# Attention probabilities divided and transposed, values as weights, in three of five attentions; one product per bank for a low-rank term

## The reference

```python
x = x + L0_attn(ln(x))           # 16 heads of 16, RoPE, tanh cap at 50, causal
x = x + L0_xattn(ln(x), ctx)     # 16 heads of 64, keys ctx[0:112] through a causal mask
x = x + L0_ffn(ln(x))            # 256-1024-256, gelu, plus low-rank terms
x = x + L1_attn(ln(x))           # 8 query heads, 2 latent key/value heads of 32, causal
x = x + L1_xattn(ln(x), ctx)     # 16 heads of 16, all 375 keys, padding mask
x = x + L1_ffn(ln(x))            # top 2 of 4 experts, each a whole encoder layer
...
m1 = (even[:, :4, :, None] * odd[:, :4, None, :]).reshape(Bx, Hx, Dx)   # from tokens 1..16
h = x @ W1.T + scale * einsum('bsd,bhd->bsh', x, m1) + b1
```

## Time and profile before

| | us |
|---|---|
| median of three runs (lowest, highest) | 3894.98 (3891.59, 3895.25) |
| the profiled execution | 3896.07 |
| its span in the trace | 3894.4 |

### The profile page before, as it was taken

The page is one execution under the profiler, slowest core; times in us unless marked ns, Lnnn a source line. Parts: engine busy times, 40 slices in busy tenths (PEclk is TensorE's granted clock), DMA queues, the critical chain, the costliest instruction groups (busy, mean ns, idle before and its releaser), DMA issues. The chain is left out here.

```text
span 3894.4 us, 81102 instructions
## 1 busy us (share of the span) xinstructions
PE 3612.2 (93%) x32871; PEld 2736.2 (70%) x32871; DVE 1980.3 (51%) x5378; ACT 1434.1 (37%) x3167; POOL 371.6 (10%) x455
## 2 busy tenths in 40 slices
PE   6999999999699898989898989994899999999997
PEld 4777777777576666666666666662788887878886
DVE  3665656566235353535353534452455555556554
ACT  2343344334134233333333343432344443444443
POOL 1111111111000000000000000000011111111111
PEclk9999999999699999999999999997899999999999
DMA  2000000000200001010101010001300001110000
GB/s 76 12 12 13 14 12 12 14 14 8 88 11 13 24 11 25 9 27 9 28 5 31 1 35 1 25 1 54 129 16 12 11 17 50 54 52 12 15 12 8
DMA packets 63555, 94.55 MB, mean 24 GB/s; under 512 B 7762, under 2 KB 59602, under 8 KB 62146
## 3 DMA queue, kind: packets, MB, share of 16 engines
q1 hardware_dynamic: 55074, 83.41, 6.9%
q0 software_dynamic: 8224, 7.36, 1.7%
HBM read 72.07 MB, written 18.37 MB: 23 GB/s over the span
## 5 line engine op out<-in xcount | busy, mean ns | idle before, releaser
L1478 PE MATMUL bps<-BXT,Bwexp 128*128 128x112 f32 x3072 | 379.7, 282 | 6.2 <-DMA Bwexp<-in_we 3.6
L1478 PEld LDWEIGHTS bps<-BXT,Bwexp 128*128 128x128 f32 x3072 | 361.7, 195 | 22.1 <-issue 9.3
L1243 DVE CUSTOM_DVE_ANT_0 PON<-pps,PMR 112x375 f32<-112x375 f32 x512 | 259.7, 544 | 194.3 <-PE pps L967 192.9
L1096 ACT ACTIVATE PPT<-pps,mcol 125x896 f32<-125x896 f32 x192 | 192.4, 1007 | 204.6 <-PE pps L986 204.4
L1564 PE MATMUL bps<-Bwexp,BPT 128*112 128x256 f32 x1024 | 235.9, 380 | 0.0
L657 POOL TENSOR_TENSOR rstd<-var,nhalf 112x1 f32<-112x1 f32 (+1 forms) x96 | 148.3, 1545 | 838.6 <-DVE var L575 459.1
L967 PE MATMUL pps<-PKT,PQM 64*112 64x375 f32 x1024 | 211.1, 501 | 6.0 <-DVE Pmx L1243 4.0
L1276 POOL TENSOR_TENSOR Prstd<-Pvar,nhalf 112x1 f32<-112x1 f32 x128 | 70.1, 548 | 1517.9 <-DVE Pvar L1164 1517.9
L1618 ACT ACTIVATE BPT<-bps,Bwexp 128x112 f32<-128x112 f32 x512 | 139.1, 354 | 170.9 <-PE bps L1478 170.9
L1564 PEld LDWEIGHTS bps<-Bwexp,BPT 128*112 128x112 f32 x1024 | 174.5, 177 | 35.3
L986 PE MATMUL pps<-PQM,PKT 64*125 64x448 f32 x768 | 187.5, 567 | 0.0
(11 more groups left out here) (302 smaller groups left out, 7280.8 us busy)
## 6 DMA issues: line engine op xcount, KB each, us to landing
Bwexp<-in_we SPq DMA_DIRECT2D x7, 2304.0 KB, 17.0
PCX<-in_ctx SPq DMA_DIRECT2D x32, 375.0 KB
BXIN<-xmid SPq DMA_DIRECT2D x64, 112.0 KB
out<-BY POOLq DMA_DIRECT2D x64, 112.0 KB, 2.9
Bwexp<-in_we SPq DMA_DIRECT2D x7, 777.0 KB, 4.6
wa_sb<-in_wa SPq DMA_DIRECT2D x1, 4736.0 KB, 14.8
Brexp<-in_re SPq DMA_DIRECT2D x7, 672.0 KB
XIN<-in_x SPq DMA_DIRECT2D x32, 112.0 KB
```

Of the source, the lines that this page charges most:

```text
L1096: A(PT[s][0:KP, k, :, :].rearrange("p (i v) q -> p i (v q)", i=2), PS[s][0:KP, :, 0:QW], ACT.Exp, bias=mcol[:, k, bass.ds(at.n[s] + s * qu ...
L1243: m = v.tensor_tensor_reduce(out=ON[s][0:T, i * LC:(i + 1) * LC], in0=bank[s][i][0:T, 0:LC], in1=MR[s][:, :], scale=1.0, scalar=-3.0e38, o ...
L1478: m = mm(o[:, j * T:(j + 1) * T], wt[:, c, n0 + j * 128:n0 + (j + 1) * 128], rhs[:, c, :], start=(c == 0), stop=(c == 1))
```

## The change

All three attentions now go the same way, eight heads at a time: scores with queries on the partitions; row maxima on DVE; one exponential for each head on ACT, with the negated maximum as bias and the row's sum as second output (`accum_out`); DVE divides the 112 x 896 probabilities; PE transposes them, ACT copies them; PE multiplies with V as weights and the probabilities moving, which gives the output with features on the partitions. In L0_xattn and L1_attn DVE adds the mask and takes the maximum in one instruction for each head (`tensor_tensor_reduce`), and PE's mask product goes. The transposes of the output go, and in L1_attn and the experts the selecting products and the second scores too. `V48` holds V of two heads with 16 columns of zeros between, so that two products of 32 output rows fill one group of rows. In L0_ffn the tiles of f1 are taken in another order, so that bank g needs one and the same 96-row operand, and the four products become one of 448 columns.

```diff
-    "lead2": (0, 66, 241, 415),
+    "lead2": (0, 341, 505, 677),
...
             t.wait(xf_read[s], 2)
         else:
             t.wait(tp_ready[s])
-        for i in range(2):
-            mm(bank[s][i][0:T, 0:QW], identb, causalb, start=True, stop=True)
         for n in range(4):
             for i in range(2):
                 m = mm(bank[s][i][0:T, n * T:(n + 1) * T], QT[s][side[i], 4 * g + n, :], KX[s][side[i], 4 * g + n, :],
-                       start=False, stop=True, skip_group_check=True)
+                       start=True, stop=True)
         m.then_inc(s_psum[s], 1)
         yield
         t.wait(soft_ready[s])
...
         m.then_inc(pt_psum[s], 1)
         yield
         t.wait(pt_ready[s])
-        for i in range(2):
-            for n in range(4):
-                m = mm(bank[s][i][0:T, 65 * n:65 * n + 65], PT[s][:, 8 + 4 * i + n, :],
-                       V64[s][:, 8 * g + 2 * n + i, :], start=True, stop=True)
+        for n in range(4):
+            for i in range(2):
+                m = mm(b0[side[i], n * T:(n + 1) * T], V64[s][:, 8 * g + 2 * n + i, :], PT[s][:, 8 + 4 * i + n, :],
+                       start=(n == 0), stop=True, skip_group_check=True)
         m.then_inc(o_psum[s], 1)
-        yield
-        t.wait(on_ready[s])
-        transposes(b0, ON[s][:, 512 * g:512 * g + 512], 4).then_inc(tp_psum[s], 1)
...
-        t.wait(sub_ready[s])
-        A(PT[s][:, 0:8, :], PT[s][:, 0:8, :], ACT.Exp).then_inc(soft_ready[s], 1)
+        t.wait(top_ready[s])
+        for h in range(8):
+            m = A(PT[s][:, h, :], PT[s][:, h, :], ACT.Exp, bias=low[s][:, h:h + 1], accum_out=sums[s][:, h:h + 1])
+        m.then_inc(sum_ready[s], 1)
         yield
         t.wait(pt_psum[s])
         A(PT[s][:, 8:16, :].rearrange("p (i n) q -> p i (n q)", i=2), PS[s][0:T, :, 0:QW],
           ACT.Copy).then_inc(pt_ready[s], 1)
         yield
-        copy_transposed(OT[s][:, 4 * g:4 * g + 4, :], b0)
+        t.wait(o_psum[s])
+        A(OT[s][:, 4 * g:4 * g + 4, :], b0[:, 0:QW].rearrange("p (n q) -> p n q", n=4), ACT.Copy).then_inc(tp_ready[s], 1)
...
-        top = mx[s][:, 8 * g:8 * g + 8]
-        scores = PS[s][0:T, :, 0:QW].rearrange("p i (n k) -> p i n k", n=4)
...
+        for i in range(2):
+            for n in range(4):
+                h = 4 * i + n
+                m = v.tensor_tensor_reduce(out=PT[s][:, h, :], in0=bank[s][i][0:T, n * T:(n + 1) * T], in1=causalb[:, 0:T],
+                                           scale=1.0, scalar=-3.0e38, op0=ALU.add, op1=ALU.max, accum_out=mx[s][:, h:h + 1])
+        chained(m)
+        v.tensor_scalar(low[s][:, :], mx[s][:, 0:8], -1.0, None, ALU.mult).then_inc(top_ready[s], 1)
+        yield
+        t.wait(sum_ready[s])
+        chained(v.reciprocal(rec[s][:, 0:8], sums[s][:, :]))
+        v.tensor_tensor(PT[s][:, 0:8, :], PT[s][:, 0:8, :], rec[s][:, 0:8].unsqueeze(2).to_broadcast((T, 8, T)),
+                        ALU.mult).then_inc(soft_ready[s], 1)
...
     def hidden(g):
         for j in range(4):
             for c in range(C2):
-                mm(bank[s][g][:, j * T:(j + 1) * T], f1[:, c, (4 * g + j) * 128:(4 * g + j + 1) * 128], XT[s][:, c, :],
+                mm(bank[s][g][:, j * T:(j + 1) * T], f1[:, c, (2 * j + g) * 128:(2 * j + g + 1) * 128], XT[s][:, c, :],
                    start=(j == 0 and c == 0), stop=False, skip_group_check=True)
         if g == 0:
             t.wait(g_ready[s])
-        for j in range(4):
-            mt = 4 * g + j
-            m = mm(bank[s][g][:, j * T:(j + 1) * T], XN[s][0:32, (mt % 2) * 128:(mt % 2) * 128 + 128], GS[s][:, mt // 2, :],
-                   start=False, stop=True, skip_group_check=True)
+        m = mm(bank[s][g][:, 0:QW], XN[s][0:96, g * 128:(g + 1) * 128], GS[s][:, :, :], start=False, stop=True, skip_group_check=True)
...
-        mm(b1[0:32, 64:64 + T], XT[s][:, c, 1:33], XT[s][:, c, :], start=(c == 0), stop=(c == 1), skip_group_check=True)
+        mm(b1[0:96, 64:64 + T], XT[s][:, c, 1:97], XT[s][:, c, :], start=(c == 0), stop=(c == 1), skip_group_check=True)
...
-    second(range(0, 4))
+    second(range(0, FT, 2))
...
-    second(range(4, 8))
+    second(range(1, FT, 2))
...
     t.wait(la_ready[s], 2)
-    for i in range(2):
-        mm(bank[s][i][0:T, 0:QW], identb, causalb, start=True, stop=True)
     for n in range(4):
         for i in range(2):
             m = mm(bank[s][i][0:T, n * T:(n + 1) * T], QM[s][side[i], n // 2, n % 2, :], KL[s][side[i], n // 2, :],
-                   start=False, stop=True, skip_group_check=True)
+                   start=True, stop=True)
     m.then_inc(s_psum[s], 1)
     yield
-    t.wait(mx_ready[s])
-    mm(b0[0:16, 0:T], MXP[s][:, :], identb, start=True, stop=True).then_inc(mt_psum[s], 1)
-    yield
-    t.wait(mt_ready[s])
+    t.wait(on_ready[s])
     for n in range(4):
         for i in range(2):
-            mm(bank[s][i][0:T, n * T:(n + 1) * T], csel[:, 4 * i + n, :], MV[s][:, :],
-               start=(n == 0), stop=False, skip_group_check=True)
...
+            m = transpose(bank[s][i][0:T, n * T:(n + 1) * T], PF[s][:, 4 * i + n, :], ident[0:T, 0:T])
     m.then_inc(st_psum[s], 1)
+    t.skip(mx_ready[s], 1)
+    t.skip(small_ready[s], 1)
     yield
     t.wait(p_ready[s])
-    for h in range(8):
-        c, j = h // 4, h % 4
-        m = mm(b0[0:T, 33 * h:33 * h + 33], PF[s][:, 4 * (j // 2) + 2 * c + j % 2, :], V32[s][:, c, :], start=True, stop=True)
-    m.then_inc(o_psum[s], 1)
+    for c in range(C2):
+        for j in range(4):
+            m = mm(b0[rows[j], c * T:(c + 1) * T], V32[s][:, c, :], PF[s][:, 4 * (j // 2) + 2 * c + j % 2, :],
+                   start=(c == 0), stop=True, skip_group_check=True)
+    m.then_inc(sp_psum[s], 1)
     token_major(b1[0:KP, 0:D], CT[s][:, :, 2 * KP:3 * KP], yv, 0, D).then_inc(kv_psum[s], 1)
-    yield
-    t.wait(on_ready[s])
-    transposes(ON)
...
-    copy_max(MV[s][0:16, :], b0[0:16, 0:T])
+    t.wait(mx_ready[s])
+    for h in range(8):
+        m = A(PF[s][:, h, :], PF[s][:, h, :], ACT.Exp, bias=neg[s][:, h:h + 1], accum_out=sums[s][:, h:h + 1])
+    m.then_inc(small_ready[s], 1)
     yield
     t.wait(st_psum[s])
-    A(PF[s].rearrange("p (i n) q -> p i (n q)", i=2), PS[s][0:T, :, 0:QW], ACT.Exp).then_inc(p_ready[s], 1)
+    A(PF[s].rearrange("p (i n) q -> p i (n q)", i=2), PS[s][0:T, :, 0:QW], ACT.Copy).then_inc(p_ready[s], 1)
     yield
     t.wait(kv_psum[s])
     A(V16[s][:, 2, :, 0:16], b1[0:KP, 0:D].rearrange("p (h d) -> p h d", h=H), ACT.Copy).then_inc(kv_read[s], 1)
-    copy_transposed(OT)
+    t.wait(sp_psum[s])
+    A(OT[s][:, :, :], b0[:, 0:C2 * T].rearrange("p (c q) -> p c q", c=C2), ACT.Copy).then_inc(tp_ready[s], 1)
...
-            t.wait(mx_ready[s])
+            t.wait(exp_ready[s])
         for v in range(4):
             for i in range(2):
                 m = mm(bank[s][i][0:T, v * T:(v + 1) * T], QM[s][side[i], c, v, :], KT[s][side[i], c, :], start=True, stop=True)
         m.then_inc(s_psum[s], 1)
-    yield
-    t.wait(mx_ready[s])
...
+    for c in range(C2):
+        yield
+        t.wait(soft_ready[s])
         if c == 0:
-            t.wait(mt_ready[s])
+            t.wait(exp_ready[s])
         else:
-            t.wait(p_ready[s])
+            t.wait(pt_ready[s])
         for v in range(4):
             for i in range(2):
-                mm(bank[s][i][0:T, v * T:(v + 1) * T], msel[side[i], 4 * c + v, 0:T], MXT[s][side[i], :],
-                   start=(v == 0), stop=False, skip_group_check=True)
...
+                m = transpose(bank[s][i][0:T, v * T:(v + 1) * T], PT[s][0:T, 8 * c + 4 * i + v, :], ident[0:T, 0:T])
+        m.then_inc(pt_psum[s], 1)
+    yield
+    t.wait(pt_ready[s])
+    for c in range(C2):
+        for n in range(2):
+            for k in range(4):
+                m = mm(b0[32 * k:32 * k + 32, c * T:(c + 1) * T], V48[s][:, 4 * c + k, 16 * n:16 * n + 32],
+                       PT[s][0:T, 8 * c + 2 * k + n, :], start=(c == 0 and n == 0), stop=(n == 1), skip_group_check=True)
+    m.then_inc(o_psum[s], 1)
...
-    t.wait(mt_psum[s])
-    A(MXT[s][:, :], b0[:, 0:T], ACT.Copy).then_inc(mt_ready[s], 1)
...
+    A(V48[s][:, :, :].rearrange("p k (n d) -> p k n d", n=3)[:, :, 0:3:2, :], b0[0:T, 0:D].rearrange("p (k n d) -> p k n d", k=8, n=2),
+      ACT.Copy).then_inc(vx_read[s], 1)
+    for c in range(C2):
+        yield
+        t.wait(top_ready[s])
+        for i in range(2):
+            for v in range(4):
+                h = 8 * c + 4 * i + v
+                m = A(PT[s][0:T, h, :], bank[s][i][0:T, v * T:(v + 1) * T], ACT.Exp, scale=0.25, bias=low[s][:, h:h + 1],
+                      accum_out=sums[s][:, h:h + 1])
+        m.then_inc(exp_ready[s], 1)
+    for c in range(C2):
+        yield
+        t.wait(pt_psum[s])
         A(PT[s][0:T, 8 * c:8 * c + 8, :].rearrange("p (i v) q -> p i (v q)", i=2), PS[s][0:T, :, 0:QW],
-          ACT.Exp, scale=0.25).then_inc(p_ready[s], 1)
-    yield
...
+          ACT.Copy).then_inc(pt_ready[s], 1)
+    yield
```

(3 more changed lines are left out.)

144 lines of the change are left out of this document (48 added, 96 removed), and 82 rows, old and new, of the table TURNS.

## The result

| | before | after |
|---|---|---|
| median of 4 runs, same chip | 3894.14 us (3891.59 to 3895.25) | 3747.80 us (3743.57 to 3758.23) |
| profiled execution, span | 3896.07, 3894.4 | 3746.19, 3744.5 |
| after / before | | 0.9632, interval 0.9619 to 0.9645 |

It is faster, by 146 us where 284 were forecast, and 18 us above the end of the range. The missing half is best looked at by phase. A phase begins with the first PE group of its own: L797 at 1040.76 and L1472 at 2734.74 before, L795 at 978.58 and L1459 at 2577.87 after.

The account below looks back on a forecast made before the run. PE was taken to bound all three phases, the other engines' work lying beside it. From 3896 us came off 284 of PE's work and 1 net for waits, turns and ends: 3611 profiled, 3610 median; 8-in-10 range 3545 to 3730.

Parts of the forecast that it names:

- PE's sum, 284 us: All phases: PE work saved, 95 us in phase 1, 98 in phase 2, 91 in phase 3.
- So small waits remain: 0.2 per item, 13 us: Phase 3: PE's waits in the new order cost 0.2 us per item, 13 us in all.
- The one wait that I had reckoned: Phase 3: an item's second scores wait 4.1 us for the first's exponentials; lane 0 has 4.7 us between its scores.
- Rival B: Phase 3, some in phase 1: exponentials serial on ACT, 0.51 us a head, so PE waits; 3700 us; chance 0.20.
- Filling and draining get longer: 10 us: Phase 2: lanes' leads spread to 0.677 of a round, so filling and draining take 10 us more.
- The turn of phase 1, +5: Phase 1: DVE's loop grows from 168 to 289 instructions; its turn adds 5 us.
- Rival E: Phase 1: DVE's 289-instruction loop stops at each turn as in phase 2; 37 us, 3642 us; chance 0.08.
- The turn of phase 2, -35: Phase 2: work queued ahead takes back a third of each loop turn's cost, 5 us per turn, seven turns, 35 us.
- C: Phase 2: the loop's turn costs nothing any more; 77 us on top, 3533 us; chance 0.07.
- D: PE's new products no cheaper: dear ends in phases 1 and 2, 3701 us; or dear transposes, 3727; chance 0.10 for both.
- the 1.10 in the prediction: Phase 3: selecting products and second scores taken out, 1.10 us, twice per item; set against eight transposes at 0.81.
- F: Phase 3: slower, ACT's chain of maximum, exponentials, division, transposes sets the pace; 3968 us at 0.9 a head; chance 0.03.

Follow-up runs that it names:

- new tables: Changed kernel, same code, with other tables of turns for all five engines in phase 3 alone: 3639.51 us, 0.9342.
- both new orders: Changed kernel with other tables of turns in phase 3 and phase 1's leads all shifted by 195 turns: 3613.01 us, 0.9277.
- the shifted one: Changed kernel with phase 1's leads all 195 turns further, so only the place of the loop's branch moves: 3717.57 us, 0.9557.

## Why the prediction was wrong, point by point

**PE's sum, 284 us: right in its prices, and close by phase.** L430, L424, L837 and L1505 have the places forecast. With new tables an item of phase 3 has (69.59 - 63.29)/4 = 1.58 us less work where 1.42 stood; in phase 2 a round written out has 11.4 less where 12.2 stood. The low-rank groups gave 13 us where 15 stood. PE's busy time as a whole fell by 219 us in the changed kernel and by 267 with both new orders. That the kernel with both orders takes 3613 us, where 3611 was the sum, is partly luck, as shown above.

**"So small waits remain: 0.2 per item, 13 us": the step that failed.** Measured are 4.3 us of idle PE a round, 1.1 an item, 69 in 64 items; the new tables won 105 in phase 3, the starts and ends of the lanes and PE's shorter groups with them. The one wait that I had reckoned, of the second scores for the first group's exponentials, is there and has its size: 0.9 us a round, where 0.8 stood. I took it for the only one. Left out were four others: the first transposes wait for the second group's exponentials (0.8), since these read the bank that the transposes overwrite; the product with V and the product for V wait for copies that stand behind eight heads in ACT's queue (0.7 and 1.0); and PE waits for SP's release of the weights (0.9). A step of ACT that had been one exponential of 0.91 us had become 2.63, and the order left no room for the 1.72 more. So I had asked for one consumer of the heads, and neither for the other nor for those of the steps queued behind them. Rival B had the symptom and nearly the time (3700) but by another cause, a head of 0.51, and that was not so: luck. That ACT's work, at most 12.4 us an item, lies under PE's 15.9 was true (11.7 measured) and proved nothing here. What is shown is that the order makes the waits, since other tables take them away. What share ACT's own queue has in them is argued from the timeline and not shown by a run.

**"Filling and draining get longer: 10 us": mis-sized.** A round of phase 2 is 18.1 us shorter with its turn and 14.8 without, eight rounds 145 or 118; yet the phase won 95, and 79 written out. So what lies outside the rounds grew by 40 to 50 us. The leads leave one lane alone at the end, PE idle a third of the time and then slow for it. Closing the gap won 54, of which the ends themselves are 21 to 24.

**The turn of phase 1, +5: mis-sized.** The step said that it costs PE "at most the 1.54 us in rows 3", plus 5 in all. The six turns cost 25.5 us, 12.4 before, so 13 more. With the branch at another place 24.5 us of phase 1 went. Rival E had 37 more, by a stop of DVE at its 289 instructions: too much, and DVE didn't stop. Another 14 us of phase 1 are missing. PE's waits for the new chain (its transposes for DVE's division L634 11.5 us, its product with V for ACT's copy 4.0, its scores for DVE 3.6) are 19 us, where those of the old transposes and product were 7. Most of the 11.5 lie outside 100 to 950, at the ends of the phase, where one lane is alone with its chain. This was not tried by itself.

**The turn of phase 2, -35: mis-sized.** The prediction counted seven turns; the loop turns six times. The change took 3.3 us off each by the rounds, 20 in all, and 10 by the times, where 5 each were forecast. The order did take PE's own stop away, 20.2 us of "issue" in all before and 6.3 after; what stayed is the wait for DVE after its stop of some 6 us (5.30 in the row above). Against that the rounds have 3.5 us fewer of the small waits than before, which the prediction had at nothing, so that together a round came out at 18.1 less where 12.2 + 5 were forecast.

**The rivals.** C (the turn free) was not so: six turns still cost 64. But its counter-argument was wrong too: "no order of work takes it away" was said of PE's own stop, and the new order took most of it away in phase 2, the shifted one all of it in phase 1. D (products no cheaper) was not so, in places and in time. The rule that the prediction set beside it, that larger matmuls are more efficient (the Trainium skill, Perfetto Trace Analysis, section Matmuls), agrees with the trace where like is compared with like: before, the same 896 columns take 0.97 us as eight products of 112 (L1506, 3027.05 to 3028.02) and 0.89 as two of 448 (L1524, 3025.11 to 3026.00). It doesn't decide here, since a transpose is one matmul where a float32 product is two, and eight transposes have 0.82; the 1.10 in the prediction has the eight selecting products in it. F (slower through ACT) had ACT's load as its measure, and the load never was the bound.

**Instruction fetch.** The Trainium skill (Runtime: NRT & Kernel Launch, section Instruction fetch mechanics) says that a taken branch outside the held blocks waits for a fetch. The runs agree that the stops come from the turn: PE's "issue" idle in phase 2 and DVE's 6.3 us are gone once the loop is written out. They do not show that a fetch is the reason, nor a size at which it begins; DVE's 289 instructions of phase 1 didn't stop.

## What to carry to other kernels

When a change makes one step of an engine longer, don't stop at that engine's load and at one consumer of the step: list everything that waits for it, what is queued behind it and who waits for that, and lay the order of all engines out anew with the new durations. An order that doesn't fit them can eat the whole gain: here it cost 105 us in phase 3, where the change with a fitting order won 99. With lanes at uneven leads, count the rounds and the ends apart: a gain per round can be lost where one lane runs alone. And if a loop is turned often, see which work stands ahead of its branch on the engine that bounds the kernel: in phase 1 the turn was free behind long products and cost 4 us a time behind short ones, the slower clock in it; in phase 2, written out, it was gone.

## What the hardware showed

- An activation with a sum is two rows in the profile, but its readout (0.21 to 0.26 us) laps over its own activation and the next: the pitch for 112 columns is 0.33 us with the sum and 0.24 without (eight in 2.63 and 1.88). In phase 1, where the heads are read from SBUF instead of PSUM, it is 0.37.
- The length of one idle stretch of PE doesn't tell whether the clock falls: it fell to its lower level for 3.4 or 6.8 us behind stops of 2.28, 2.36, 2.49 and 2.77 us and once behind 1.77, and not behind 2.40, 2.76 and 1.80. With the clock down, groups of 1.04 us lasted 1.79. In the last 80 us of phase 2, with PE idle a third of the time, the mean clock was 0.61.
- The same 625 matmuls of a round took PE 64.56 us with five stops among them and 63.29 without, at a granted clock of 1.00 in both.
- Code written out from end to end is not slower than loops that turn: 3534 against 3532 us, the intervals of the ratios laid over each other (0.9057 to 0.9088, 0.9044 to 0.9078).
